# Layer 1's own-key attention weights: two heads' products issued in one TensorE step

## The reference, cut to what matters

```python
q = x @ Wq.T
k = jnp.concatenate([x_text @ Wk.T, x @ Wk.T], axis=1)
v = jnp.concatenate([x_text @ Wv.T, x @ Wv.T], axis=1)
...
scores = jnp.einsum('bhnd,bhkd->bhnk', q, k) / jnp.sqrt(jnp.float32(d))
first = jnp.tanh(gate) * jnp.ones_like(scores[..., :1])
rest = jax.nn.softmax(scores[..., 1:], axis=-1)
attn = jnp.concatenate([first, rest], axis=-1)
out = jnp.einsum('bhnk,bhkd->bhnd', attn, v)
```

## Time and profile before

| | us |
|---|---|
| median of 3 runs (lowest to highest) | 927.13 (927.07 to 929.5) |
| profiled execution, its own time | 930.15 |
| its span, first to last instruction | 928.4 |
| mean granted TensorE clock over the span | 0.953 |
| TensorE busy | 841.6 |
| VectorE busy | 763.0 |
| ScalarE busy | 555.4 |
| GpSimd busy | 309.8 |

### The profile page before, as it was taken

The page is one execution under the profiler, slowest core; times in us unless marked ns, Lnnn a source line. Parts: engine busy times, 40 slices in busy tenths (PEclk is TensorE's granted clock), DMA queues, the critical chain, the costliest instruction groups (busy, mean ns, idle before and its releaser), DMA issues.

```text
span 928.4 us, 16914 instructions
## 1 busy us (share of the span) xinstructions
PE 841.6 (91%) x5288; PEld 651.5 (70%) x5288; DVE 763.0 (82%) x1907; ACT 555.4 (60%) x1077; POOL 309.8 (33%) x507
## 2 busy tenths in 40 slices
PE   5998887899999999999999999999979989978796
PEld 3776756666666665688878788778767779867574
DVE  6899899869999998699889899788887755465886
ACT  3777565547777775675666565577755534423474
POOL 2644226313444433232222122433421253321143
PEclk9999999759999997999999999999998999997998
DMA  5000000000000000010000000020001000000001
GB/s 155 9 2 1 4 26 1 25 1 26 26 25 26 22 23 1 9 42 0 1 1 1 1 1 1 0 76 2 1 2 43 1 1 1 1 1 1 1 12 34
DMA packets 26005, 14.12 MB, mean 15 GB/s; under 512 B 11047, under 2 KB 25406, under 8 KB 25918
## 3 DMA queue, kind: packets, MB, share of 16 engines
q1 hardware_dynamic: 25758, 13.04, 5.1%
q10 hardware_dynamic: 160, 0.00, 0.0%
HBM read 11.99 MB, written 1.05 MB: 14 GB/s over the span
## 4 chain that ended last, share of the span: by engine, by line
PE 47%; DVE 8%; issue 3%; ACT 3%; POOL 0%; DVEq 0%; ACTq 0%; POOLq 0%
PE bank L1844 4%; PE bank L1846 3%; PE bank L1845 3%; PE bank L798 2%; PE bank L1319 2%; PE bank L1900 2%; PE bank L1901 2%; PE bank L1899 2%; PE bank L1274 2%; PE bank L1284 2%; PE bank L1297 1%; PE bank L1255 1%; PE bank L731 1%; PE bank L709 1%; PE bank L758 1%
## 5 line engine op out<-in xcount | busy, mean ns | idle before, releaser
L893 ACT ACTIVATE L_pt<-bank 128x512 f32<-128x512 f32 x224 | 127.2, 598 | 46.4 <-PE bank L767 32.5
L515 POOL TENSOR_TENSOR L_kc<-L_kc_all,const 128x256 fp32r<-128x256 f32 x96 | 59.7, 625 | 141.7 <-PE bank L767 81.9
L1026 DVE TENSOR_REDUCE L_ms<-bank 128x2 f32<-128x512 f32 x128 | 84.0, 685 | 11.8 <-PE bank L716 11.4
L1801 POOL TENSOR_TENSOR L1f_xg_lo<-L1f_xg_raw,L1f_xg_hi 128x512 fp32r<-128x512 f32 x32 | 42.0, 1313 | 145.3 <-ACT L1f_xg_hi L1949 141.3
L880 ACT ACTIVATE L_part<-bank,L_bias_ca,const 128x256 fp32r<-128x256 f32 x128 | 68.9, 563 | 33.8 <-PE bank L687 32.4
L2065 DVE TENSOR_TENSOR L1f_h_lo<-L1f_h,L1f_h_hi 128x512 fp32r<-128x512 f32 x88 | 75.2, 859 | 6.2 <-ACT L1f_h_hi L1954 5.9
L1943 ACT ACTIVATE L1f_a<-bank 128x512 f32<-128x512 f32 x88 | 52.4, 599 | 43.3 <-PE bank L1846 42.9
L1024 DVE TENSOR_REDUCE L_mc<-bank 128x8 f32<-128x512 f32 (+1 forms) x96 | 65.1, 678 | 8.7 <-PE bank L709 4.4
L1954 ACT CAST L1f_h_hi<-L1f_h 128x512 fp32r<-128x512 f32 x88 | 54.3, 618 | 18.8 <-DVE L1f_h L2060 18.8
L716 PE MATMUL bank<-L_k,L_q 32*128 32x256 f32 x256 | 55.9, 342 | 5.1 <-DVE L_ms L1026 4.9
L887 ACT ACTIVATE L_hm<-bank,const 128x256 fp32r<-128x256 f32 x96 | 45.6, 475 | 21.5 <-PE bank L731 20.6
(11 more groups left out here) (427 smaller groups left out, 2601.1 us busy)
## 6 DMA issues: line engine op xcount, KB each, us to landing
L_raw<-in_L_ffn_w_dram SPq DMA_DIRECT2D x8, 176.0 KB, 2.3
L_raw<-in_L_ffn_v_dram SPq DMA_DIRECT2D x8, 176.0 KB, 2.5
L_raw<-in_L_ffn_w_dram SPq DMA_DIRECT2D x6, 192.0 KB, 2.9
x<-in_x_dram SPq DMA_DIRECT2D x4, 256.0 KB, 4.3
mask<-in_mask_Bx1xSxS_ff_dram SPq DMA_DIRECT2D x2, 512.0 KB, 5.6
out_dram<-x SPq DMA_DIRECT2D x4, 256.0 KB, 2.3
const<-in_const_dram SPq DMA_DIRECT2D x1, 964.0 KB, 6.0
ctx_rows<-in_ctx_dram SPq DMA_DIRECT2D x1, 256.0 KB, 3.1
```

The lines of the kernel that those rows point to most:

```text
L515: pool.tensor_tensor(kc[:, g], kc_all[:, g, bass.ds(b, 1)].bitcast(F32).to_broadcast([P, GH, S2]), pr.c("head4").unsqueeze(2).to_broadcast ...
L893: act.activation(pt[:, g // 2, (g % 2) * NS + (HEADS_1[i] if own_keys else i)], b_st[(g * NS + i) % 2][:], ACT.Exp, scale=scale).then_inc( ...
L1026: dve.tensor_reduce(ms[:, :, i - 1], bank.rearrange("p (t s) -> p t s", s=S), AX_X, ALU.max).then_inc(sem["sc_taken"], 1)
```

## The change

The steps of units 2 and 4 do nothing on TensorE. The steps of units 1 and 3 issue the products of their own head and of the next, alternating: first half of head A, first half of head B, last half of A, last half of B. As the second head's bank is that of the unit before the pair, the step waits for the exp of that unit (unit 0 for the pair 1, 2; unit 2 for the pair 3, 4), one exp more than before. `st_done` is raised once behind each head's last product, as before. Nothing changes on the other engines, and neither STEPS_1 nor PLACES does.

```diff
--- before.py
+++ after.py
@@ -733,7 +733,9 @@
 
         def weights(b, g, i):
             at = g * NS
-            need(pe, sem["exp_done"], b * U + (at + i - 1), past["exp_done"])
+            if i in (2, 4):
+                return
+            need(pe, sem["exp_done"], b * U + (at + i - (0 if i else 1)), past["exp_done"])
             o = b_st[(at + i) % 2]
             if i == 0:
                 pe.wait_ge(sem["m_split"], past["m_split"] + b * NG + g + 1)
@@ -760,11 +762,12 @@
                         pe.matmul(op, i2[:], msk_all[:, bass.ds(b, 1)].rearrange("p a s -> p (a s)"), start=False, stop=False)
                     last = pe.matmul(op, selc[:, pair], mt[:, g % 2], start=False, stop=True)
             else:
-                h = HEADS_1[i]
-                rows = slice(32 * (h - 1), 32 * h)
                 for kt in range(2):
-                    op = o[:, kt * S:(kt + 1) * S]
-                    last = pe.matmul(op, k[rows, g, kt * P:(kt + 1) * P], mt[rows, g % 2], start=True, stop=True)
+                    for j in (i, i + 1):
+                        rows = slice(32 * (HEADS_1[j] - 1), 32 * HEADS_1[j])
+                        last = pe.matmul(b_st[(at + j) % 2][:, kt * S:(kt + 1) * S], k[rows, g, kt * P:(kt + 1) * P], mt[rows, g % 2], start=True, stop=True)
+                        if kt == 1 and j == i:
+                            last.then_inc(sem["st_done"], 1)
             last.then_inc(sem["st_done"], 1)
 
         def values(b):
```

## The result

The changed kernel takes 945.24 us (median of 4 runs, 941.24 to 946.93), the kernel before beside it on the same chip 927.37 (4 runs, 927.07 to 929.5): 1.0181 times as long, with an interval of 1.0146 to 1.0217. The prediction said 933.2, in a range of 926.8 to 937.2: the direction was right, the size was not, and the result lies outside the range. The profiled execution took 945.66 us.

What follows compares the result with a forecast made beforehand. VectorE was taken to bound batches 1 to 6 of layer 1's attention, half-clock TensorE batch 0. Waits of 3.8 (batches 1 to 6), 1.8 (batch 0) and 0.5 (batch 7) add 6.1 to 927.1: 933.2 us, range 926.8 to 937.2.

Steps and rivals of the forecast that it cites:

- The order of the four products: In TensorE's pair steps: the two heads' products already overlap, a block of four stays at 0.51 us, cost and gain 0.
- six free places: Six of eight pair places per batch: TensorE arrives after the exp ends or within 0.03 us of its end, cost 0.
- Place 1: Group 0, pair (3,4), batches 1 to 7: waiting for weight 2's exp costs 0.50 us per batch, bounds 0.37 and 0.55.
- the slip of the second copy: ScalarE's second copy of the next batch's transposed x, group 0's pair (3,4): 0.50 us later, and VectorE's xt_lo waits for it.
- Place 2: Group 2, pair (1,2), batches 1 to 6: VectorE gets the maxima copy late, 0.13 us per batch, bounds 0 and 0.25.
- Batch 0: Batch 0, TensorE the bound: three steps wait longer for exps, 1.8 us taken, bounds 0 to 2.3.
- Batch 7: Last batch: group 0's pair (3,4) wait once more, other effects cancel; 0.5 us, bounds -0.5 to 1.0.
- rival 4: Clock falls elsewhere or later rises: delayed products thin TensorE's work, one batch at half clock costs 10.4, 943.6 us; chance 0.10.
- T: Theory stated with the experiments, not in the prediction: the clock's falls follow from a TensorE that is thinner filled; no size.
- C: Theory stated with the experiments, not in the prediction: clock falls are chance, differing between runs without regard to the kernel.
- Rivals 1 to 3: 1: waits cost nothing, merging pays, 921.3, chance 0.10; 2: delays absorbed, 928, 0.12; 3: batch 0's clock rises earlier, 928.1, 0.10.

Runs made afterwards that it cites:

- first experiment: Changed kernel with the products inside a pair step in the old order, head A's two then head B's two, waits kept; 946.08 us, ratio 1.0181.
- eighth experiment: Changed kernel merged only in batches 1 to 6, at the six places where the exp is over when TensorE arrives; 929.21 us, ratio 0.999.
- 2, place 1 apart: Changed kernel with group 0's pair (3,4) split into separate steps again, with the waits of before; 937.87 us, ratio 1.0093.
- 3, places 1 and 2 apart: Changed kernel with group 0's pair (3,4) and group 2's pair (1,2) both split again, with the waits of before; 937.42 us, ratio 1.0094.
- 6, before, both fillers: Kernel before plus eight unread products per batch, batches 1 to 7: four before group 0's weights 3, four before group 3's scores step 4; 933.1 us, ratio 1.0037.
- 5, changed, both fillers: Changed kernel plus eight unread products per batch, batches 1 to 7: four before group 0's pair (3,4), four before group 3's scores step 4; 936.28 us, ratio 1.0067.
- 9, filler at place 1: Changed kernel plus four unread products per batch, batches 1 to 7, ahead of group 0's pair (3,4) only; 940.17 us, ratio 1.0099.
- 10, filler at scores step 4: Changed kernel plus four unread products per batch, batches 1 to 7, ahead of group 3's scores step 4 only; 942.04 us, ratio 1.0129.
- 4, the wait alone: Kernel before, its steps and order kept, with units 1 and 3 waiting one exp longer; 948.51 us, ratio 1.0197.

## Why the prediction was wrong

**The order of the four products: right.** 0 predicted; the first experiment gives 946.08 against 945.24, and blocks of four take 0.50. The products of the second head overtook those of the first already.

**The six free places: right.** The eighth experiment, 0.999.

**Place 1: right in mechanism, a little high.** 0.50 per batch predicted within 0.37 and 0.55, measured 0.41. The term that was too large is the slip of the second copy. Timeline of ScalarE in the kernel before, the exps of units 3 and 4 and the copies behind them:

```profile
283.83 1.09 ACT L893 ACTIVATE L_pt<-bank 128x512 f32<-128x512 f32 x2
284.94 0.37 ACT L865 COPY L_xt_raw<-bank 128x256 f32<-128x256 f32 x1
285.21 0.38 ACT L866 CAST L_xt_hi<-bank 128x256 fp32r<-128x256 f32 x1
```

From the block of four (282.12 before, 289.88 after) the exp of unit 3 slips from 1.71 to 2.20, by 0.49 as forecast; the second copy from 3.09 to 3.43, by only 0.34. The first copy now starts 0.11 before the exps end (293.06 against 292.08 + 1.09), before it started 0.02 after them; why, the rows don't say. xt_lo slips by 0.36 (3.50 to 3.86).

**Place 2: right in mechanism, a little low.** 0.13 predicted within 0 and 0.25, 0.2 by experiments 2 and 3. The two together, 0.63, measured 0.6: that they agree so well is luck, one was 0.09 too high and the other 0.07 too low.

**Batch 0: right within its bounds.** 1.8 predicted within 0 and 2.3, 1.4 in the profile. Batch 7's 0.5 was not measured by itself.

**The step that failed is rival 4 and the place it was given.** The prediction wrote: "The before run holds 1.00 over all of them. Chance 0.10", left the rival outside the range, and put the clock at nothing in the sum. The rows it rested on were of one execution, at full clock, and say nothing of how near TensorE is to losing it. It did name the mechanism ("Delayed products thin out TensorE's work in batches 1 to 6"), but as an alternative to the waits. It goes with them: the same wait that delays VectorE leaves TensorE idle, and inside this stage the clock took about 8.9 of the 15.5 us. More than half of that, about 5.3, lies behind the xt_lo of batch 6, where the kernel before falls too (at 360.2 for 10.2 us and at 377.3 for 3.4); the prediction had no term for these falls.

At place 1 it looks like this. In the ten microseconds before the third xt_lo (a stretch picked for reading, no property of the chip) TensorE was busy 9.89 us before:

```profile
226.25:236.25 10.00, 9.89 (x92) 7.11 (x84) 9.39 (x25) 7.97 (x18) 1.96 (x3) 1.00 0.00 0
```

With the change it is 9.28. The 0.61 between them is the 0.60 that TensorE waits at place 1. Over all profiled kernels of the argument, with the time at half clock in batches 1 to 6 (up to the last xt_lo) and from there to the end of the stage:

```
kernel                            ratio    busy of 10 us   half clock, us: batches 1-6   behind
before                            1             9.89                        0             13.7
8, six free places                0.999         9.88                        3.4           10.2
6, before, both fillers           1.0037        9.92                        0              3.4
5, changed, both fillers          1.0067        9.88                        0              3.4
2, place 1 apart                  1.0093        9.88                        0             13.7
3, places 1 and 2 apart           1.0094        9.88                       13.7           17.1
9, filler at place 1              1.0099        9.88                        3.4           13.7
10, filler at scores step 4       1.0129        9.27                        0             44.4
changed                           1.0181        9.28                       10.2           30.7
1, changed, old order             1.0181        9.27                       10.2           30.7
4, the wait alone                 1.0197        9.31                        3.4           27.3
```

The four kernels with 9.3 us have the four highest ratios and 27.3 to 44.4 us at half clock behind batch 6; the others have 3.4 to 17.1. In batches 1 to 6 the column does not separate them: kernel 3 has most falls there and kernel 10 none. That fillers take the clock's part away with the waits left as they are (experiment 5, ten runs) shows that this part comes from what TensorE is given to do and not from the waits on VectorE: T stands for the kernels as wholes, though not for the place of a single fall. C, chance without regard to the kernel, does not: the changed kernel and the first experiment, on other executions, fall at the same places and for as long, and have a mean clock of 0.934 to 0.944 in all 8 runs, while the kernel before has 0.948 or more in every run beside a kernel of the experiments. Within one kernel, though, the executions do differ: the kernel before alone ran from 923.09 to 934.11 on one chip.

A second, smaller step was the size: one batch wholly at half clock (10.4 us) was taken as the price of rival 4. What came were stretches of 3.4 to 10.2 us, 10.2 us of them in batch 2 for 3.6 us of time, and 17.0 more than before behind the xt_lo of batch 6 (30.7 against 13.7) for about 5.3. Half clock priced at 0.30 us per us was about right: 0.35 and 0.31. That the rival's 943.6 comes near 945.24 is luck: its one batch of 10.4 stands for several stretches, most of them elsewhere, and for the 0.9 in layer 0.

**Rivals 1 to 3** fell: the period is longer by all of the waits (no gain, nothing absorbed), and batch 0's half-clock stretch is 34.1 us long in both kernels.

**What stays open:** what exactly tips the clock, since identical batches of one execution, each with 9.3 us in the ten before xt_lo, keep it or lose it, and kernel 3 loses it in batches whose steps are those of before; whether one group of fillers would do at some other position; whether the fillers act by their work alone or also by shifting what stands behind them; and how much of experiment 3's remainder is the waits of batches 0 and 7 and how much their clock.

## What to carry to other kernels

Merging two steps of an in-order engine makes both wait for the later of their conditions; find the places where the engine arrives before it, and price everything queued behind, which here came out right to 0.1 us per place and batch. Then ask what the new idle time does to TensorE's clock: where a kernel is already seen falling to half clock now and then, a wait on TensorE should be priced twice, and the range should reach to the case in which it falls once or twice more. Where a stretch sits at half clock though TensorE seems busy, try products that nobody reads in the places where it waits; 35 of them gave 10 us in the profiled execution and about 6 in the median. In a place where TensorE hardly waits they only cost: 0.43 us per batch in experiment 6.

## What the runs showed of the hardware

- **A busy share of 96% in the profile did not bring the clock back.** Batch 0 before has TensorE busy 33.68 of 35.0 us and stays at the lower level, 1.2 GHz, for 34.1 us, while batch 4 holds 1.00 with 22.92 of 24.6. At the lower level the products themselves take longer, which fills the busy time; that time alone doesn't tell which level is granted. With 35 products of 128 rows x 256 columns added, batch 0 ran at 1.00 in the profiled execution. Whether it is the added time or the number of rows that counts was not separated.
- **The fall needs no long gap.** In the changed kernel it came at 245.9, within a run of full-array products 0.12 apart. In the twenty microseconds before it TensorE's longest idle times are the 0.60 us of place 1, which end at 237.4, and this one of 0.54 us:

```profile
243.66 0.50 PE L716 MATMUL bank<-L_k,L_q 32*128 32x256 f32 x2 [0.54 <-DVE L_ms L1029]
244.09 0.66 PE L818 MATMUL bank<-const,L_ot 128*128 128x128 f32 x4
244.67 0.50 PE L768 MATMUL bank<-L_mt,L_k 32*128 32x256 f32 x4
245.10 0.50 PE L709 MATMUL bank<-L_kc,L_q 128*128 128x256 f32 x2
245.44 0.28 PE L685 MATMUL bank<-L_xt_hi,L_wx 128*128 128x256 f32 x1
245.56 0.28 PE L686 MATMUL bank<-L_xt_lo,L_wx 128*128 128x256 f32 x1
245.68 0.29 PE L687 MATMUL bank<-L_xt_hi,L_wx 128*128 128x256 f32 x1
245.81 0.36 PE L685 MATMUL bank<-L_xt_hi,L_wx 128*128 128x256 f32 x1
245.96 0.42 PE L686 MATMUL bank<-L_xt_lo,L_wx 128*128 128x256 f32 x1
246.18 0.41 PE L687 MATMUL bank<-L_xt_hi,L_wx 128*128 128x256 f32 x1
```

  From 245.96 on the starts are 0.22 apart in place of 0.12. The Trainium skill, "TensorE: Matmul & The Clock Gate", section "A second HAM failure mode: psum-queue depth-cycling", tells of a kernel whose many short idle moments between groups of matmuls make the clock swing between its two levels. This trace agrees as far as it goes: the idle times ahead of the fall are many and short, 0.6 us at most. The page's kernel cycles through banks of PSUM; whether the cause here is the same no run shows.
- **Products on other rows overtake.** The two products of one head, on the same 32 rows, start 0.22 apart, while four of two heads take 0.50 us, whether they are written A, A, B, B or A, B, A, B. In the block at 282.12 of the kernel before, written A, A, B, B, the starts are 282.117, 282.124, 282.340 and 282.347, and the two that raise `st_done`, the last of A and the last of B, are the third and the fourth to start: B's first began before A's last.
